# Staging W1 per batch as the stationary operand, and seeding one batch in four on ScalarE, in a conditional adapter with layer norm

## The reference

```python
w1, w2 = W1[ids], W2[ids]
h = relu(einsum('bsh,bha->bsa', x, w1) + b1[ids])
y = x + einsum('bsa,bah->bsh', h, w2) + b2[ids]
normed = (y - mean(y)) * rsqrt(var(y) + 1e-5)
out = x + normed * gamma[ids] + beta[ids]
```

## Time and profile before

| what | value |
|---|---|
| median of 3 runs | 325.59 us (325.28 to 325.63) |
| span of the profiled execution | 323.8 us |
| own time of the profiled execution | not given apart from the runs' 325.28 to 325.63 |
| PE busy | 301.9 us, 93% |
| DVE busy | 307.6 us, 95% |
| ACT busy | 230.4 us, 71% |
| POOL busy | 185.7 us, 57% |
| DMA | 75.69 MB, mean 234 GB/s |
| TensorE's granted clock, mean | 0.969 |

### The profile page before, as it was taken

One profiled execution on the slowest core, in us unless ns is written; L12 is line 12 of the kernel. 1 busy time (PEld: TensorE's weight loads), 2 busy tenths in 40 slices (PEclk: granted clock), 3 DMA queues, 4 the chain that ended last, 5 costly groups with the idle time before them and its releaser, 6 DMA issues. The chain is left out here.

```text
span 323.8 us, 8068 instructions
## 1 busy us (share of the span) xinstructions
PE 301.9 (93%) x2200; PEld 272.8 (84%) x2200; DVE 307.6 (95%) x679; ACT 230.4 (71%) x541; POOL 185.7 (57%) x217
## 2 busy tenths in 40 slices
PE   1659999999999999999999999999999999999962
PEld 1239899999999999999999999999999999999941
DVE  5687999999999999999999999999999999999996
ACT  3956677777777777877778777787777877778752
POOL 2960755556655566555665556655566555665553
PEclk9877999999999999999999999999999999999995
DMA  5999988766766667676776676766667666433324
GB/s 160 302 356 428 379 291 273 236 228 231 257 232 227 228 229 263 223 233 226 230 256 232 228 231 227 261 236 221 231 225 262 221 234 232 160 132 134 130 108 152
DMA packets 41711, 75.69 MB, mean 234 GB/s; under 512 B 2253, under 2 KB 7404, under 8 KB 41542
## 3 DMA queue, kind: packets, MB, share of 16 engines
q1 hardware_dynamic: 41571, 75.04, 68.5%
q10 hardware_dynamic: 99, 0.14, 0.1%
HBM read 41.62 MB, written 33.55 MB: 232 GB/s over the span
## 5 line engine op out<-in xcount | busy, mean ns | idle before, releaser
L295 POOL TENSOR_TENSOR x_io<-x_io,beta_all 128x512 f32<-128x512 f32 x128 | 161.2, 1280 | 0.0
L401 PE MATMUL ps_h<-w_all,x_T 128*128 x1024 | 137.0, 284 | 0.0
L401 PEld LDWEIGHTS ps_h<-w_all,x_T 128*128 128x128 f32 x1024 | 126.1, 194 | 1.6
L345 ACT ACTIVATE cut<-ps_y,row_sum 128x512 bf16<-128x512 f32 x128 | 88.0, 688 | 24.0 <-PE ps_y L428 24.0
L572 DVE SCALAR_TENSOR_TENSOR x_io<-ps_y,rstd,x_io 128x512 f32<-128x512 f32 x128 | 90.2, 747 | 2.5 <-DVE rstd L564 0.3
L559 DVE SCALAR_TENSOR_TENSOR ps_y<-ps_y,mean,gamma_all 128x512 f32<-128x512 f32 x128 | 90.8, 754 | 0.8 <-ACT cut L345 0.6
L292 POOL TENSOR_TENSOR mean<-row_sum,over_h 128x2 f32<-128x2 f32 x64 | 12.9, 201 | 125.6 <-DVE ps_y L540 113.6
L540 DVE SCALAR_TENSOR_TENSOR ps_y<-x_io,b_all 128x512 f32<-128x512 f32 x124 | 83.1, 713 | 0.0
L393 PE MATMUL ps_T<-identity,x_io 128*128 128x128 f32 x512 | 68.2, 277 | 10.0 <-DMA x_io<-in_x 10.0
L393 PEld LDWEIGHTS ps_T<-identity,x_io 128*128 128x128 f32 x512 | 61.1, 143 | 19.1 <-issue 10.4
L322 ACT COPY x_T<-ps_T 128x1024 f32<-128x1024 f32 x64 | 63.7, 995 | 8.2 <-PE ps_T L393 8.2
(11 more groups left out here) (60 smaller groups left out, 173.6 us busy)
## 6 DMA issues: line engine op xcount, KB each, us to landing
x_io<-in_x SPq DMA_DIRECT2D x64, 512.0 KB, 4.4
out<-x_io SPq DMA_DIRECT2D x63, 512.0 KB, 3.0
x_io<-in_L_cond_W SPq DMA_DIRECT2D x5, 512.0 KB, 7.2
w_all<-in_L_cond_W SPq DMA_DIRECT2D x5, 512.0 KB, 8.9
b_all<-in_L_cond_b SPq DMA_DIRECT2D x1, 2560.0 KB, 15.7
out<-x_io SPq DMA_DIRECT2D x2, 256.0 KB, 2.0
x_io<-in_L_cond_gamma SPq DMA_DIRECT2D x1, 60.0 KB
x_io<-in_L_cond_beta ACTq DMA_DIRECT2D x1, 60.0 KB
```

The source lines that it names most:

```text
L295: nc.gpsimd.tensor_tensor(x_slot(t), x_slot(t), of_lang(beta_all, langs[b]), ALU.add)\
L345: nc.scalar.activation(squares[:, t % 2, :], ps_y[t % Y_BANKS][:, :], ACT.Square, scale=-float(H), bias=stat(row_sum, t), accum_out=stat(s ...
L401: last = nc.tensor.matmul(part, x_T[:, t % 4, c, :], w1_all[:, bass.ds(lang, 1), c, :].rearrange("p o a -> p (o a)"), start=False, stop=(c ...
```

## The change

The second operand order of the first product: W1 becomes the stationary operand and x_T the moving one, so that h comes out already turned. For this the W1 of each batch is copied by DMA to a fixed place (`w1_stage`, four pairs), for the first six pairs from HBM, later from `w1_all` in SBUF. SP issues these two copies per pair with the place in a register, six pairs ahead, after the first product of the pair that used the place before. `turn_h`, `copy_h` and `h_rows` are gone; two banks `ps_h` take their place, and ScalarE's relu writes `h_high` directly. b1 is put in for both batches by one matmul of 256 columns with `is_lang`, a table of which language each batch has (built once on DVE from an iota of POOL). One batch in four (t = 7, 11, ..., 127, the second of each odd pair) is seeded by ScalarE with x alone, and PE adds b2, centred over H beforehand by ScalarE, by a matmul of 512 columns (L486). The ring of x shrinks from 12 to 10 pairs, FIRST from 3 to 2 (PE takes the second product one step earlier), `low_h` stands behind the seeds, and the queue loads in another order at the start: the first stagings, W2 and x(1) ahead of `w1_all`.

```diff
-SLOTS = 24
+SLOTS = 20
-H_PAIRS = 6
-FIRST = 3
+H_PAIRS = 3
+STAGE_PAIRS = 4
+STAGE_AHEAD = 6
+STAGE_HBM = 6
+FIRST = 2
...
+        def by_scalar(t):
+
+            return t % 4 == 3 and t >= 2 * EARLY
...
+            def stage_w1(q):
+
+                langs = langs_of(sp, q)
+                if q >= STAGE_PAIRS:
+                    sp.wait_ge(h_summed, q - STAGE_PAIRS + 1)
+                if q >= STAGE_HBM:
+                    sp.wait_ge(s_w1, 16 * W_CHUNKS)
+                table = w1_rows if q < STAGE_HBM else w1_all
+                for b in range(2):
+                    sp.dma_start(w1_stage[:, 2 * (q % STAGE_PAIRS) + b, :, :], table[:, bass.ds(langs[b], 1), :, :])\
+                        .then_inc(w1_staged[q % STAGE_PAIRS], 16)
+
+            sp.wait_ge(ids_ready, 1)
+            stage_w1(0)
+            load_w2(0)
+            load_w2(1)
+            load_x(1)
+            stage_w1(1)
+            for n in range(2, W_CHUNKS):
                 load_w2(n)
+            load_x(2)
+            stage_w1(2)
+            sp.dma_start(b2_all[:, :, :], b2.partition_broadcast(128)).then_inc(s_b2, 16)
+            load_x(3)
+            stage_w1(3)
             for n in range(W_CHUNKS):
                 langs = slice(n * LC, (n + 1) * LC)
+                sp.dma_start(w1_all[:, langs, :, :], w1_rows[:, langs, :, :]).then_inc(s_w1, 16)
+            sp.wait_ge(gamma_parts_ready, 1)
+            sp.wait_ge(beta_parts_ready, 1)
             for p in range(4, X_FIRST):
                 load_x(p)
+            for q in range(STAGE_PAIRS, STAGE_AHEAD):
+                stage_w1(q)
             for n in range(W_CHUNKS):
                 sp.wait_ge(w2_low_ready, (n + 1) * LC)
                 load_x(X_FIRST + n)
 
             for p in range(PAIRS - 1):
+                if p + STAGE_AHEAD < PAIRS:
+                    stage_w1(p + STAGE_AHEAD)
                 sp.wait_ge(out_ready, 2 * p + 2)
...
+            def mean_of_pair(n):
+                wait_seed(pool, 2 * n)
+                wait_seed(pool, 2 * n + 1)
+                nc.gpsimd.tensor_tensor(stats(neg_mean, n), stats(row_sum, n), neg_over_h[:, 0:2], ALU.mult)\
+                    .then_inc(mean_ready, 1)
...
+            def seed(t):
+
+                act.wait_ge(x_loaded[t // 2 % X_PAIRS], x_loads(t // 2))
+                act.wait_ge(out_ready, t - Y_BANKS + 1)
+                nc.scalar.activation(ps_y[t % Y_BANKS][:, :], x_slot(t), ACT.Identity,
+                                     accum_out=stat(row_sum, t)).then_inc(seeded_act, 1)
+
             def step(p):
 
                 if p < PAIRS - 1:
                     copy_x(p + 1)
-                if p > 0:
-                    high_h(p - 1)
-                copy_h(p)
+                t = 2 * (p - FIRST) + 3
+                if by_scalar(t):
+                    seed(t)
+                high_h(p)
...
+            def first_products(p):
+
+                bank = pair_of(ps_h[p % 2])
+                if p >= 2:
+                    pe.wait_ge(h_low_ready, p - 1)
+                nc.tensor.matmul(bank.rearrange("a (b s) -> a b s", b=2), b1_parts[:, :],
+                                 is_lang[:, 2 * p:2 * p + 2].unsqueeze(2).broadcast_to([128, 2, S]), start=True, stop=True)
+                pe.wait_ge(w1_staged[p % STAGE_PAIRS], 32 * (p // STAGE_PAIRS + 1))
                 for b in range(2):
+                    for c in range(C):
+                        last = nc.tensor.matmul(bank[:, b * S:(b + 1) * S],
+                                                w1_stage[:, 2 * (p % STAGE_PAIRS) + b, c, :],
+                                                x_T[:, (2 * p + b) % 4, c, :],
+                                                start=False, stop=False, skip_group_check=True)
+                last.then_inc(h_summed, 1)
...
-                pe.wait_ge(seeded, t + 1)
+                wait_seed(pe, t)
+                if by_scalar(t):
+                    nc.tensor.matmul(bank, is_lang[:, t:t + 1].broadcast_to([128, S]), parts[:, 2 * H:3 * H],
+                                     start=False, stop=False, skip_group_check=True)
...
-                if p is not None:
-                    low_h(p)
                 if n + 2 < PAIRS:
                     seed_pair(n + 2, langs[n + 2])
+                    low_h(n + 2)
```

More of the change, by code:

```diff
@@ L41, in build @@
     by_dve = [n for n in range(2 * L) if n not in by_act]
[L42 removed]
+    assert FIRST + 1 <= H_PAIRS
     with ExitStack() as ctx:
@@ L96, in build @@
         ps_T = psum("ps_T", [128, 2, C, S], F32)
-        ps_h = psum("ps_h", [128, H], F32)
-        ps_hT = psum("ps_hT", [128, H], F32)
+        ps_h = [psum(f"ps_h{i}", [128, H], F32) for i in range(2)]
         ps_y = [psum(f"ps_y{i}", [128, H], F32) for i in range(Y_BANKS)]
@@ L107, in build @@
         s_w1 = sem("s_w1")
+        w1_staged = [sem(f"w1_staged{i}") for i in range(STAGE_PAIRS)]
         s_w2 = [sem(f"s_w2_{n}") for n in range(W_CHUNKS)]
@@ L163, in spread_to, with scalar_seeds, vector_seeds, wait_seed @@
             return (gamma_all if n < L else beta_all)[:, n % L, :]
+        def by_scalar(t):
+            return t % 4 == 3 and t >= 2 * EARLY
+        def scalar_seeds(t):
+            return len([u for u in range(t + 1) if by_scalar(u)])
+        def vector_seeds(t):
+            return t + 1 - scalar_seeds(t)
+        def wait_seed(engine, t):
+            if by_scalar(t):
+                engine.wait_ge(seeded_act, scalar_seeds(t))
+            else:
+                engine.wait_ge(seeded, vector_seeds(t))
         def x_slot(t):
@@ L302, in _ @@
             for n in range(PAIRS):
-                add_beta(n)
+                langs = langs_of(pool, n)
+                mean_of_pair(n)
+                for b in range(2):
+                    add_beta(2 * n + b, langs[b])
         @block.scalar
@@ L381, in _ @@
                 step(p)
-            square_pair(PAIRS - FIRST)
-            high_h(PAIRS - 1)
-            for n in range(PAIRS - FIRST + 1, PAIRS):
+            for n in range(PAIRS - FIRST, PAIRS):
                 square_pair(n)
+                if n + 1 < PAIRS and by_scalar(2 * n + 3):
+                    seed(2 * n + 3)
         @block.tensor
@@ L395, in turn_x @@
                 last.then_inc(x_turned, 1)
-            def first_product(t, lang):
-                part = pair_of(ps_h)[:, (t % 2) * A:(t % 2 + 1) * A]
-                nc.tensor.matmul(part, of_lang(pick, lang), b1_parts[:, :], start=True, stop=False)
-                for c in range(C):
-                    last = nc.tensor.matmul(part, x_T[:, t % 4, c, :],
-                                            w1_all[:, bass.ds(lang, 1), c, :].rearrange("p o a -> p (o a)"),
-                                            start=False, stop=(c == C - 1))
-                if t % 2 == 1:
-                    last.then_inc(h_summed, 1)
-            def turn_h(p):
-                pe.wait_ge(h_rows_ready, p + 1)
-                if p > 0:
-                    pe.wait_ge(h_low_ready, p)
-                for b in range(2):
-                    last = nc.tensor.transpose(pair_of(ps_hT)[:, b * S:(b + 1) * S], h_rows[:, p % 2, b, :],
-                                               identity[:, :])
-                last.then_inc(h_turned, 1)
+            def first_products(p):
[5 more added lines that the diff above has]
+                pe.wait_ge(w1_staged[p % STAGE_PAIRS], 32 * (p // STAGE_PAIRS + 1))
+                for b in range(2):
+                    for c in range(C):
[4 more added lines that the diff above has]
+                last.then_inc(h_summed, 1)
             def put_b2(t, lang):
@@ L465, in _ @@
                     turn_x(2 * p + 3)
-                if p > 0:
-                    turn_h(p - 1)
-                for b in range(2):
-                    first_product(2 * p + b, langs[p][b])
+                first_products(p)
                 if p < PAIRS - 1:
@@ L528, in low_h @@
                 dve.wait_ge(h_high_ready, p + 1)
-                nc.vector.scalar_tensor_tensor(flat(h_low[:, p % H_PAIRS, :, :]), pair_of(ps_hT), 1.0,
-                                               flat(h_high[:, p % H_PAIRS, :, :]).bitcast(F32), ALU.mult, ALU.subtract)\
+                nc.vector.scalar_tensor_tensor(flat(h_low[:, p % H_PAIRS, :, :]), pair_of(ps_h[p % 2]), 0.0,
+                                               flat(h_high[:, p % H_PAIRS, :, :]).bitcast(F32), ALU.max, ALU.subtract)\
                     .then_inc(h_low_ready, 1)
```

120 lines of the change are left out of this document (63 added, 57 removed).

## The result

The changed kernel takes **329.93 us** (median; 328.94 to 331.58) against 325.58 for the kernel before: ratio 1.0145, 95% interval 1.0116 to 1.0174. It is slower by 4.4 us, where 3.1 us of gain was forecast.

What follows compares the result with a forecast made beforehand. PE was taken as the bound at 4.49 us per pair, DVE right behind. Start -2.5, x(4) and x(5) +1.8, 61 periods of 4.425 -3.3, end +0.9: together -3.1, giving 322.5 us; range 313 to 332.

Steps and rivals of the forecast that it cites:

- collision: Steady stretch: DVE seeds and POOL's beta additions exclude each other, period 4.425 us per pair, 319.5 to 325.5; chance 0.45.
- larger losses or a worse start: Rival: DVE blocked twice per pair, later x loads or PE waits at W1 stagings; 325 to 330 us, chance 0.14.
- PE: Steady stretch: PE's work per pair falls from 4.49 to 4.33 us.
- the b2 matmul: Added on PE in every second pair: 0.23 to 0.38 us per two pairs, 0.15 per pair.
- DVE: Steady stretch: one seed of four goes, so DVE's own work falls from 4.43 to 4.12 us per pair.
- rival 1: Steady stretch: seeds meeting beta additions cost little, so PE's 4.33 us per pair rules; 314.4 us, chance 0.28.
- 94% of 4.425: covered: Steady DMA queue: 1.57 MB per pair at 379 GB/s needs 4.15 us, within the period with little room.
- Rival 2: Steady stretch: the DMA queue becomes the bound; 338 us at 250 GB/s, 377 at twice the price; chance 0.13.
- decides from about 4.6 per pair: Steady DMA queue: it sets the time from this period on, when SBUF copies run below about 286 GB/s.
- First T: T is the start of a pair's first second product; the first was forecast at 32.5 instead of 35.01, saving 2.5 us.
- x(4) and x(5) +1.8: Start: PE waits 1.3 us for x(4), landing at about 39.6, and another 0.5 for x(5).
- End: From pair 61's second product to the end of the span: 16.5 us, 0.9 more than before.

Runs made afterwards that it cites:

- half_split_start: start_and_split, but from pair 6 on only the first batch's W1 of each pair is copied, the second batch using an old W1; 316.64 us (one execution).
- no_beta_add: Changed kernel with POOL's two beta additions per pair replaced by a write of one column each, all copies kept; 324.85 us (one execution).
- extra_copy: Kernel before with a ring of 10 pairs and, per pair, four unread 256 KB copies within SBUF added; 417.96 us (one execution).
- no_act_seed: Changed kernel with every seed back on VectorE and no b2 matmul; 327.58 us, ratio 1.0047.
- hbm_rows_nosplit: hbm_rows with the beta additions in the changed kernel's order, both behind both seeds; 323.58 us, ratio 0.9941.
- half_collide: Changed kernel with its own start and addition order, but from pair 6 on only the first batch's W1 is copied; 329.85 us (one execution).
- hbm_rows_again: The same kernel as hbm_rows, measured in a second comparison with more rounds beside hbm_rows_noseed; 323.78 us, ratio 0.9841.
- start_order: Changed kernel with x(4), x(5) and the stagings of pairs 4 and 5 put between the loads of w1_all; 331.68 us, ratio 1.0186.
- start_and_split: Changed kernel with the edits of both start_order and pool_split; 327.74 us, ratio 1.0062.
- hbm_rows: Changed kernel without the W1 table, every W1 staged from HBM in 2 KB rows, additions split as in pool_split; 321.49 us, ratio 0.9764.
- pool_split: Changed kernel with POOL adding beta to a pair's first batch before waiting for ScalarE's seed of the second; 328.61 us, ratio 1.0061.
- hbm_rows_noseed: hbm_rows_nosplit with every seed on VectorE and no b2 matmul; 323.42 us, ratio 0.9877.

## Why the prediction was wrong

**Direction.** Forecast faster with 0.70; it is slower, ratio 1.0145. The time lies within the range of 313 to 332 only because the range took in the rivals; the 319.5 to 325.5 given for the collision alone is missed. It is near the rival of "larger losses or a worse start" (325 to 330, 0.14).

**PE.** Forecast 4.33, measured 4.16 and 4.40 in turn, 4.29 where nothing holds it (half_split_start). The step was right and slightly too cautious: the b2 matmul costs 0.24 per two pairs, the low end of what I gave.

**DVE.** Forecast 4.12 plus a collision. With all seeds on DVE it needs 4.42 to 4.43, as read from the earlier trace rows.

**The collision.** The step held part by part. From a T (209.19) ScalarE's seed ends at +4.31 (forecast 4.35), POOL adds from +4.60 (4.58) to +7.11 (7.09), the next T but one is at +8.90 (8.85). The bet that a DVE seed with PSUM output excludes a beta addition like L523 did was right, and the cheap collision (rival 1, 0.28) is refuted: a seed takes 941 ns for 713 before, and 704 in no_beta_add, where the additions are gone. The Trainium skill's rule quoted in the prediction (SBUF — State Buffer, section Who interferes with whom) agrees with these numbers. The term was undersized by 0.035 us per pair, 2.1 us in all: from h_low's end to T it is 0.25 instead of 0.1, of which the seeds give some back (1.13 behind POOL's end instead of 1.26).

**DMA.** "94% of 4.425: covered" took 379 GB/s from one microsecond early in the run. Over windows of 40 us the mix moves 342 to 349 in the changed kernel, 344 to 351 in extra_copy when full, at most 358 in no_act_seed, so the share is not 94% but about 100%. The 379 was not a stray value but another mix: loads alone, in rows of 2 KB, move 385 over the 16 us from 24 to 40 in hbm_rows_nosplit. That did not make the changed kernel slow by itself (half_collide), but it removed every reserve: whoever mends the start or the collision runs into it. Rival 2 (the queue as the bound) is not what made the changed kernel slow, but its limit is real, and "decides from about 4.6 per pair" was wrong: the queue begins to take at 4.4 to 4.5.

**Start.** First T forecast 32.5, measured 31.98: right. "x(4) and x(5) +1.8" is **the step that failed**. It had the right count of data (12.7 MB ahead, 13.2 with x(4)), but took the pace of the kernel before, 13.2 MB by 40.5. By the windows the changed kernel has moved as much only at 42.7, and x(4) is there at 43.15. The sum also put it at 39.6, although by its own rate 13.2 MB are in at 40.5. In the stretch from 32 to 40 us the queue moves 296 GB/s at full share, against 372 in the same 8 us before. The table in rows of 512 bytes comes in just there; the other runs with a table there have 290 to 314 in this stretch. The kernels without it, with every W1 in rows of 2 KB, have 379 to 385, save hbm_rows_again, whose queue runs short there (315). That it is the rows and nothing else in that order of loads is argued from these windows; no run changes the rows alone. And the sum had no price for the clock: a PE that waits 3.95 us loses another 2.54 at 1.2 GHz. What was taken as 1.8 is 7.5: 3.95 of waiting, 2.54 and 1.40 at the low clock, less what a pair takes under the forecast's 4.425 here (4.18). x(5) kept nothing waiting (4.31 from pair 2 to pair 3). hbm_rows_nosplit, which has no table at the start but the same collision, has no gap: 8.52 us from pair 0 to pair 2, less than the forecast's 10.65, and a span of 320.8 (320.7 was forecast; it has 2.1 less there and as much more in the steady stretch, so that the two agree is luck).

**End.** 16.55 for 16.5.

**The late first T.** It falls at 31.9 to 32.6 in some executions and at 33.7 to 35.7 in others, with the table or without it, and start_order and start_and_split, which load in the same order, have 34.79 and 32.28. The traces show the same collision once more, at the start. The last two `w_low` instructions of VectorE, which read two SBUF tensors, meet POOL's first beta additions. In hbm_rows_nosplit VectorE is first, in the profiled execution of hbm_rows_again POOL is:

```profile
30.95 1.41 DVE L590 SCALAR_TENSOR_TENSOR w_low<-x_io,w_neg_mean,w_high 128x512 fp32r<-128x512 f32 x2
31.71 3.04 POOL L344 TENSOR_TENSOR x_io<-x_io,beta_all 128x512 f32<-128x512 f32 x2
```

```profile
32.11 2.94 POOL L344 TENSOR_TENSOR x_io<-x_io,beta_all 128x512 f32<-128x512 f32 x2
32.68 2.91 DVE L596 SCALAR_TENSOR_TENSOR w_low<-x_io,w_neg_mean,w_high 128x512 fp32r<-128x512 f32 x2 [0.87 <-ACT w_high L393]
```

| run | sixteen W1 passes of pair 0 | last two w_low | first T |
|---|---|---|---|
| hbm_rows | 2.32 | 1.41 | 32.46 |
| hbm_rows_nosplit | 2.50 | 1.41 | 32.50 |
| after | 2.73 | 1.41 | 31.98 |
| pool_split | 3.25 | 2.44 | 33.68 |
| hbm_rows_noseed | 3.34 | 3.50 | 34.44 |
| start_order | 3.61 | 3.31 | 34.79 |
| half_split_start | 3.62 | 3.25 | 34.91 |
| hbm_rows_again | 3.62 | 2.91 | 35.73 |
| no_beta_add | 3.62 | 1.42 | 32.62 |

In the runs in which PE does these passes at the low clock for longer, ScalarE's last `w_high` comes later, and VectorE finds POOL already adding. no_beta_add, where POOL adds nothing, settles it: its passes are as slow as any, and still `w_low` takes 1.42 and the first T is at 32.62. Where `w_low` is late, PE idles 3.2 to 4.3 us for it and begins pair 0 at the low clock, and the step to pair 1 takes 5.5 to 7.0 us (5.58 in the changed kernel, after 2.45 of idling).

**What stays open:** why the low clock lasts through these passes in some executions and not in others. And what the queue's limit would be with fewer, larger descriptors, and whether bytes or the number of copies fill it: this was not tried.

## What to carry to other kernels

Price a transfer by the rate of a long stretch that is full, in the same mix, not by a microsecond of the start: between 379 GB/s and the 342 to 349 of the steady stretch lay the whole reserve. A late load early in the run costs its wait and then the clock: here 3.95 us of waiting became 6.5. And when the removal of a loss changes nothing, relieve the next resource before judging: half of the copies away told in two runs that the collision sets the steady period, and that the full queue would keep the gain of mending it. After an edit to the order of loads, follow the start to the last pair that it touches: start_and_split had no gap up to pair 4 and a gap of 5.9 us behind it.

## What the hardware showed

- A DVE instruction with two SBUF inputs and a PSUM output waits for the end of the two-input POOL addition that it meets, as one with an SBUF output does: 1.42 to 1.71 us instead of 0.70, and 2.91 to 3.50 instead of 1.41 for two `w_low`.
- A copy from SBUF to SBUF is worth its bytes once, not twice: with 1 MB more per pair the queue moved 344 to 351 GB/s at full share (extra_copy), each copied byte counted once.
- How long a load holds SP depends on what stands before it: loads of 512 KB took from 0.46 to 6.07 us to issue. While W1 came in rows of 512 bytes, the queue moved 290 to 314 GB/s at the start, in rows of 2 KB 379 to 385 where it was full.
- A transpose whose fp32 input is every fourth column of x is nearly free: 4.24 per pair instead of 4.16 to 4.18, for eight of them.
